# A two-layer graph network on one core: where VectorE doubles the low part, and the order of a step around it

## The chip, the core and the metric

The kernel runs on one core of a Trainium2 chip. The time is the device time of one execution in microseconds, from the kernel's median of several runs; the trace comes from one profiled execution, whose clock starts with its first instruction. TensorE does the matrix products, VectorE, ScalarE and GpSimd the element-wise work, SyncE issues the loads and stores. Each engine runs its own list of instructions in order, and semaphores tie the lists together.

## What is computed

128 graphs of 64 nodes with 512 features in fp32, and one adjacency matrix of 64 x 64:

```python
x = layernorm(x + einsum('bnf,nm->bmf', x, adj * adj) + bias)
z_l, z_g, v = x @ W_lang.T, x @ W_grav.T, x @ W_V.T
A_l = max(cosine(z_l, z_l), 0) * not_eye
A_g = exp(-dist2(z_g, z_g) / (2 sigma**2)) * not_eye
K = w_l * rownorm(A_l * adj) + (1 - w_l) * rownorm(A_g * adj)
x = layernorm(x + (K @ v) @ W_O.T)
```

## The kernel before

The 128 graphs go through in 16 groups of 8 (512 rows, as four tiles of 128 x 512), one group g a step. A step is a software pipeline: while it computes the projections, the Gram matrices and K of group g, it also brings group g+1 through the first layer and its transposes, and closes group g-1 (K·u, the sum with the residual, the second layer norm, the store). The order on each engine is written out by hand in a function `step(g)` for each engine, with a prologue before step 0 and a last step written out separately. Nothing plans it: an instruction that waits holds everything behind it on its engine.

Products are made in three terms from a high and a low part of each operand (hi·hi, hi·lo, lo·hi). So each transposed tile of the normalised y is kept three times: `hT` (the full value, copied by ScalarE, `copy_hT`), `hT_hi` (rounded, by ScalarE, `hi_hT`) and `hT_lo` (their difference, by VectorE, `lo_hT`, L780). The buffers alternate between two groups.

TensorE's step: the products 0 to 3 of the projections (L388), the two halves of layer 0 of group g+1 (`layer0`, L348) alternating with the two halves of K·u of group g-1 (`apply_k`, L439), products 4 to 8, the transposes of tiles 0 and 1 of group g+1 (`transpose_h`, L361), the Gram products (`gram`, L407), then products 9, 10, 11 with the transposes of tiles 2 and 3 between, and two small transposes of the inverse norms (`rows`, L419). Products 8 to 11 are u, the product with the folded W_V and W_O. Three PSUM banks form a ring for the products; ScalarE empties them (`evict`). The last tile of layer 0 sits in a ring bank too, and product 6 is the next to take that bank, once VectorE has added the bias (`add_y`, L764). The second half of K·u writes the banks that the first two of these additions read.

`gram(g)` multiplies `hT` with the projections. For its first chunk it needs hT + hT_lo in place of hT, which VectorE makes in place (`double_lo`, L786) and counts in `hT_doubled`; gram waits for it at L395. In the kernel before VectorE does it for group g+1 at the end of step g, behind `turn_k(g)` (L880, K's transposition) and in front of `add_y(g + 2, 0)`.

VectorE's step begins with the additions of y and z (`add_y`, `add_z` L886) and their statistics (`count_y`, `count_z` L891, `gather_z` L900). Then it waits for ScalarE's copy of P, gram's result (`copy_p`), and goes down a long chain: `diagonals` (L791), `lo_hT` of tiles 0 and 1, `shift`, `turn_p` (L815), `lo_hT` of tiles 2 and 3, `add_p` (L822), `weigh` (L831, needs TensorE's `rows`), `coefficients`, `combine`, `turn_k`. GpSimd makes the scale and offset of the layer norms from the statistics (`scale_y`, `scale_z`, with L1079 to L1084) and the inverse norms (`columns`); ScalarE applies them (`normalise_h`, `normalise_out`).

Of the kernel before, what the change touches and what calls it, by code (L numbers as in the profile page):

```python
# [5 lines left out]
def bass_two_layer_graph_resnorm(  # L6
# [64 lines left out]
    with ctx:  # L71
# [243 lines left out]
        def _(pe):  # L315
# [127 lines left out]
            def step(g, tail=True):  # L443
                project(g, 0)
                project(g, 1)
                project(g, 2)
                project(g, 3)
                layer0(g + 1, 0)
                if tail:
                    apply_k(g - 1, 0)  # L450
                layer0(g + 1, 1)
                if tail:
                    apply_k(g - 1, 1)
                project(g, 4)
                project(g, 5)
                project(g, 6)
                project(g, 7)
                project(g, 8)
                transpose_h(g + 1, 0)
                transpose_h(g + 1, 1)  # L460
                gram(g)
                project(g, 9)
                transpose_h(g + 1, 2)
                project(g, 10)
                transpose_h(g + 1, 3)
                project(g, 11)
                rows(g)
# [85 lines left out]
            g = NG - 1  # L553
# [20 lines left out]
        def _(act):  # L574
# [8 lines left out]
            def normalise_h(g, p):  # L583
                act.wait_ge(y_scale, 2 * g + p // 2 + 1)
                act.activation(h_sb[g % 3][:, p, :], h_sb[g % 3][:, p, :], ACT.Identity, scale=y_rs[:, p:p + 1],  # L585
                               bias=y_nb[:, p:p + 1]).then_inc(h_ready, 1)
# [33 lines left out]
            def step(g, tail=True):  # L620
                evict(g, 0)
                evict(g, 1)
                evict(g, 2)
                evict(g, 3)
                evict(g, 4)
                evict(g, 5)
                normalise_h(g + 1, 0)
                normalise_h(g + 1, 1)
                evict(g, 6)
                evict(g, 7)  # L630
                normalise_h(g + 1, 2)
                evict(g, 8)
                if tail:
                    normalise_out(g - 1, 0)
                hi_hT(g + 1, 0)
                copy_hT(g + 1, 0)
                copy_p(g)
                hi_hT(g + 1, 1)
                normalise_h(g + 1, 3)
                copy_hT(g + 1, 1)  # L640
                evict(g, 9)
                copy_hT(g + 1, 2)
                evict(g, 10)
                hi_hT(g + 1, 2)
                hi_hT(g + 1, 3)
                copy_hT(g + 1, 3)
                if tail:
                    normalise_out(g - 1, 1)
                exp_g(g)
                if tail:  # L650
                    normalise_out(g - 1, 2)
                    normalise_out(g - 1, 3)
                evict(g, 11)
# [73 lines left out]
            g = NG - 1  # L727
# [23 lines left out]
        def _(dve):  # L751
# [151 lines left out]
            def step(g, tail=True):  # L903
                add_y(g + 1, 0)
                add_y(g + 1, 1)
                if tail:
                    add_z(g - 1, 0)
                    count_z(g - 1, 0)
                add_y(g + 1, 2)
                if tail:  # L910
                    add_z(g - 1, 1)
                    count_z(g - 1, 1)
                add_y(g + 1, 3)
                if tail:
                    gather_z(g - 1, 0)
                    add_z(g - 1, 2)
                count_y(g + 1, 0)
                count_y(g + 1, 1)
                if tail:
                    add_z(g - 1, 3)  # L920
                    count_z(g - 1, 2)
                    count_z(g - 1, 3)
                diagonals(g)
                lo_hT(g + 1, 0)
                lo_hT(g + 1, 1)
                shift(g)
                turn_p(g)
                if tail:
                    gather_z(g - 1, 1)
                lo_hT(g + 1, 2)  # L930
                lo_hT(g + 1, 3)
                add_p(g)
                weigh(g)
                coefficients(g)
                combine(g)
                turn_k(g)
                double_lo(g + 1)

            def blocks_of_ident():
                dve.wait_ge(ident_ready, 2)  # L940
# [85 lines left out]
            lo_hT(0, 2)  # L1026
            lo_setup(13)
            lo_hT(0, 3)
            double_lo(0)
            lo_setup(14)  # L1030
            lo_setup(15)

# [1 line left out]
            for g in range(1, NG - 1):  # L1034
                step(g)
            g = NG - 1
            add_z(g - 1, 0)
            count_z(g - 1, 0)
            add_z(g - 1, 1)
# [5 lines left out]
            add_p(g)  # L1045
            weigh(g)
            coefficients(g)
            add_z(g - 1, 3)
            combine(g)
            gather_z(g - 1, 0)  # L1050
            turn_k(g)
            count_z(g - 1, 2)
            count_z(g - 1, 3)
            gather_z(g - 1, 1)
            add_z(g, 0)
            add_z(g, 1)
            count_z(g, 0)
            count_z(g, 1)
            add_z(g, 2)
            gather_z(g, 0)  # L1060
# [11 lines left out]
        @block.gpsimd  # L1072
        def _(pool):
            def scale_of(stats, ve_done, rs_done, scale, mv, ve, nm, rs, nb, d, h):

                pq = slice(2 * h, 2 * h + 2)
                pool.wait_ge(stats, d + 1)
                settle(pool)
                pool.tensor_scalar(ve[:, pq], mv[:, pq, 1], LN_EPS, None, ALU.add).then_inc(ve_done, 1)  # L1079
                pool.wait_ge(ve_done, d + 1)  # L1080
                pool.tensor_tensor(rs[:, pq], ve[:, pq], pow_neg_half[:, 0:2], ALU.pow).then_inc(rs_done, 1)
                pool.tensor_scalar(nm[:, pq], mv[:, pq, 0], -1.0, None, ALU.mult).then_inc(rs_done, 1)
                pool.wait_ge(rs_done, 2 * d + 2)
                pool.tensor_tensor(nb[:, pq], nm[:, pq], rs[:, pq], ALU.mult).then_inc(scale, 1)  # L1084

            def scale_y(g, h):
                scale_of(y_stats, y_ve_done, y_rs_done, y_scale, y_mv, y_ve, y_nm, y_rs, y_nb, 2 * g + h, h)

            def scale_z(g, h):
                if g > 0:  # L1090
                    pool.wait_ge(o_ready, NP * g - NP + 2 * h + 2)
                scale_of(z_stats, z_ve_done, z_rs_done, z_scale, z_mv, z_ve, z_nm, z_rs, z_nb, 2 * g + h, h)

            def columns(g):
                pool.wait_ge(sq_done, g + 1)
                settle(pool)

                pool.tensor_scalar(sq_floor[:, :].rearrange("r (h a) -> r h a", a=2), sq[:, :, L, :], EPS * EPS, None,
                                   ALU.max).then_inc(floor_done, 1)
                pool.wait_ge(floor_done, g + 1)  # L1100
                pool.tensor_tensor(inv_norm[:, :], sq_floor[:, :], pow_neg_half[:, :], ALU.pow).then_inc(inv_done, 1)
                pool.tensor_scalar(sq_eps[:, :], sq_floor[:, :], 2 * EPS, None, ALU.mult).then_inc(sq_eps_done, 1)
                pool.wait_ge(inv_done, g + 1)
                pool.tensor_copy(inv_rep[:, :, :], inv_norm[:, :].unsqueeze(2).broadcast_to([R, NP, N])).then_inc(
                    inv_ready, 1)
                pool.wait_ge(sq_eps_done, g + 1)
                pool.tensor_tensor(floors[:, L, :], sq_eps[:, :], inv_norm[:, :], ALU.mult).then_inc(floors_ready, 1)

            def step(g, tail=True):
                scale_y(g + 1, 0)  # L1110
                scale_y(g + 1, 1)
                if tail:
                    scale_z(g - 1, 0)
                columns(g)
                if tail:
                    scale_z(g - 1, 1)

            pool.memset(ident[:, :], 0.0).then_inc(ident_ready, 1)
            pool.wait_ge(ident_ready, 1)
            pool.affine_select(out=ident[:, :], in_=ident[:, :], compare_op=ALU.not_equal, fill=1.0, base=0,  # L1120
                               pattern=[[-1, R]], channel_multiplier=1).then_inc(ident_ready, 1)
            pool.memset(pow_neg_half[:, :], -0.5)
            pool.memset(floors[:, G, :], EPS).then_inc(pow_ready, 1)
            pool.wait_ge(pow_ready, 1)
            for h in range(2):
                scale_y(0, h)
            step(0, tail=False)
            for g in range(1, NG - 1):
                step(g)
            g = NG - 1  # L1130
            columns(g)
            scale_z(g - 1, 0)
            scale_z(g - 1, 1)
            scale_z(g, 0)
            scale_z(g, 1)
# [27 lines left out]
```

## Time and profile before

| | before |
|---|---|
| median of 3 runs | 600.31 us (599.86 to 600.78) |
| the profiled execution | 600.05 us, span 598.2 us |
| TensorE busy | 578.7 us (97%), clock 0.995 of full |
| VectorE busy | 439.0 us (73%) |
| ScalarE busy | 292.1 us (49%) |
| GpSimd busy | 141.2 us (24%) |
| one step | about 34.3 us |

"Busy" adds up the times in which an engine has an instruction under way. The ends of matrix products are modelled and overlap with the next one's start, so distances between starts say more about TensorE than durations do. PEld is TensorE's weight load.

### The profile page before, as it was taken

How to read it: one execution, taken by the hardware profiler on the slowest of the kernel's cores; microseconds unless marked ns; L12 is line 12 of the kernel's file. 1: busy time of each engine (PE TensorE's matmuls, PEld its weight loads, DVE VectorE, ACT ScalarE, POOL GpSimd, SP SyncE). 2: the span in 40 equal slices, each digit the busy share in tenths (PEclk: the TensorE clock that was granted, in tenths of full speed). 3: DMA queues.
4: the chain of work that ended last, by engine and by line, in shares of the span. 5: the costliest groups of instructions: out<-in, count | busy, mean ns of one | idle time of the engine just before them, and what ended most of it. 6: DMA issues, size and time to landing. Idle time of an engine off the chain costs nothing.

```text
span 598.2 us, 10012 instructions
## 1 busy us (share of the span) xinstructions
PE 578.7 (97%) x3681; PEld 443.2 (74%) x3681; DVE 439.0 (73%) x1022; ACT 292.1 (49%) x516; POOL 141.2 (24%) x344
## 2 busy tenths in 40 slices
PE   7999999999999999999999999999999999999991
PEld 5887868686886868688686868778686868868770
DVE  4843795959689595959769595967959595886586
ACT  4644426365463635456362645546263644636413
POOL 0201113032232304123230313223130412323013
PEclk9999999999999999999999999999999999999997
DMA  8713030411313040131304022131303110100003
GB/s 297 196 21 70 1 71 19 96 46 54 89 53 71 26 116 20 54 87 55 71 37 105 19 85 58 54 85 58 71 19 108 35 54 19 53 1 37 36 0 140
DMA packets 20783, 38.67 MB, mean 65 GB/s; under 512 B 2176, under 2 KB 2176, under 8 KB 20736
## 3 DMA queue, kind: packets, MB, share of 16 engines
q1 hardware_dynamic: 20736, 38.05, 22.4%
q8 instruction: 29, 0.48, 0.3%
q14 instruction: 18, 0.15, 0.1%
HBM read 21.27 MB, written 16.78 MB: 64 GB/s over the span
## 4 chain that ended last, share of the span: by engine, by line
PE 61%; DVE 27%; ACT 5%; issue 4%; DMA 1%; SPq 0%; DVEq 0%; POOL 0%; POOLq 0%
PE ring L388 42%; PE bank_s L407 10%; DVE KT L880 5%; DVE h_sb L764 3%; DVE X L831 3%; PE bank_y L439 3%; ACT hT_hi L576 2%; PE bank_y L361 2%; DVE XW L860 2%; DVE sums L845 2%; DVE hT_lo L780 2%; DVE S L822 2%; PE ring L513 1%; ACT u_sb L576 1%; PE bank_z L361 1%
## 5 line engine op out<-in xcount | busy, mean ns | idle before, releaser
L576 ACT ACTIVATE yT<-ring 128x512 f32<-128x512 f32 x128 | 71.0, 592 | 141.5 <-PE ring L388 141.4
L388 PE MATMUL ring<-hT_hi,T_hi 128*128 128x512 f32 x320 | 127.7, 399 | 0.0
L388 PE MATMUL ring<-hT_hi,T_lo 128*128 128x512 f32 x320 | 124.8, 390 | 0.0
L388 PE MATMUL ring<-hT_lo,T_hi 128*128 128x512 f32 x288 | 112.3, 390 | 0.0
L388 PE MATMUL ring<-M_hi,hT_hi 128*128 128x512 f32 x256 | 104.5, 408 | 0.0
L388 PE MATMUL ring<-M_hi,hT_lo 128*128 128x512 f32 x256 | 100.4, 392 | 0.0
L388 PE MATMUL ring<-M_lo,hT_hi 128*128 128x512 f32 x256 | 99.8, 390 | 0.0
L791 DVE TENSOR_TENSOR diag_scr<-P_sb,ident_c 128x512 f32<-128x512 f32 x16 | 11.1, 692 | 103.4 <-ACT P_sb L576 103.4
L388 PEld LDWEIGHTS ring<-hT_hi,T_hi 128*128 128x128 f32 x320 | 60.0, 188 | 23.8 <-issue 12.2
L1079 POOL TENSOR_SCALAR y_ve<-y_mv 128x2 f32<-128x2 f32 x32 | 7.7, 239 | 266.2 <-DVE y_mv L774 265.0
L585 ACT ACTIVATE h_sb<-h_sb,y_nb,y_rs 128x512 f32<-128x512 f32 x64 | 50.4, 810 | 39.6 <-POOL y_nb L1084 39.6
L388 PEld LDWEIGHTS ring<-hT_hi,T_lo 128*128 128x128 f32 x320 | 60.1, 188 | 12.8
L388 PEld LDWEIGHTS ring<-hT_lo,T_hi 128*128 128x128 f32 x288 | 54.2, 188 | 10.4
L576 ACT ACTIVATE u_sb<-ring 128x512 f32<-128x512 f32 x64 | 37.7, 590 | 44.6 <-PE ring L388 44.6
L407 PE MATMUL bank_s<-yT,hT 128*64 128x128 f32 x1024 | 59.4, 274 | 0.0
L407 PEld LDWEIGHTS bank_s<-yT,hT 128*64 128x64 f32 x1024 | 55.6, 137 | 3.3 <-issue 1.8
L815 DVE STREAM_TRANSPOSE P_turned<-P_sb 32x256 f32<-32x256 f32 x128 | 55.8, 436 | 2.0
L388 PEld LDWEIGHTS ring<-M_hi,hT_hi 128*128 128x128 f32 x256 | 48.1, 188 | 11.8 <-issue 3.4
L388 PEld LDWEIGHTS ring<-M_hi,hT_lo 128*128 128x128 f32 x256 | 48.0, 188 | 10.7
L388 PEld LDWEIGHTS ring<-M_lo,hT_hi 128*128 128x128 f32 x256 | 48.2, 188 | 8.7
L617 ACT ACTIVATE h_sb<-h_sb,z_nb,z_rs 128x512 f32<-128x512 f32 x63 | 49.6, 811 | 8.0 <-POOL z_nb L1084 7.9
L780 DVE TENSOR_TENSOR hT_lo<-hT,hT_hi 128x512 fp32r<-128x512 f32 x64 | 42.3, 680 | 4.5 <-ACT hT L576 4.2
(135 smaller groups left out, 849.0 us busy)
## 6 DMA issues: line engine op xcount, KB each, us to landing
x_sb<-in_x_dram SPq DMA_DIRECT2D x32, 512.0 KB, 6.4
out_dram<-h_sb SPq DMA_DIRECT2D x60, 256.0 KB, 2.0
yT<-in_L_gnn_W_lang_dram SPq DMA_DIRECT2D x4, 256.0 KB, 3.1
yT<-in_L_gnn_W_grav_dram SPq DMA_DIRECT2D x1, 1024.0 KB, 7.4
h_sb<-in_L_gnn_W_V_dram SPq DMA_DIRECT2D x1, 1024.0 KB, 11.0
h_sb<-in_L_gnn_W_O_dram SPq DMA_DIRECT2D x1, 1024.0 KB, 12.4
out_dram<-h_sb SPq DMA_DIRECT2D x8, 128.0 KB, 2.4
bias_bc<-in_L_gnn_bias_dram SPq DMA_DIRECT2D x1, 256.0 KB, 8.2
```

The lines of the kernel that those rows point to most:

```text
L361: last = pe.transpose(hT_bank[p][:, s], h_sb[g % 3][:, p, s], ident[:, :])
L388: last = pe.matmul(ring[ring_of(g, k)][:, :], a, b, start=n == 0, stop=n == len(terms) - 1)
L407: last = pe.matmul(p_ps[half(a), h, :, c, :], hT[g % 2][:, i, t], yT[:, i, :, t], start=i == 0, stop=i == DC - 1, tile_position=(0, a * N))
L439: last = pe.matmul(z_bank(2 * h + a)[half(c), :], KT[half(a), h, half(c)], u_sb[half(a), 2 * h + c, :], start=True, stop=True, tile_positi ...
L576: return act.activation(dst, src, ACT.Copy, scale=scale)
L585: act.activation(h_sb[g % 3][:, p, :], h_sb[g % 3][:, p, :], ACT.Identity, scale=y_rs[:, p:p + 1], bias=y_nb[:, p:p + 1]).then_inc(h_ready, 1)
L617: act.activation(h_sb[g % 3][:, p, :], h_sb[g % 3][:, p, :], ACT.Identity, scale=z_rs[:, p:p + 1], bias=z_nb[:, p:p + 1]).then_inc(o_ready, 1)
L764: dve.tensor_tensor(h_sb[g % 3][:, p, :], y_bank(g, p)[:, :], bias_bc[:, :], ALU.add).then_inc(y_added, 1)
L780: dve.tensor_tensor(hT_view(hT_lo[g % 2], p), hT_view(hT[g % 2], p), hT_view(hT_hi[g % 2], p), ALU.subtract).then_inc(hT_split, 1)
L815: last = dve.transpose(P_turned[col:col + B, :, i * B:(i + 1) * B], P_sb[row:row + B, :, :, :, j * B:(j + 1) * B].rearrange("r h s a j -> ...
L831: last = dve.scalar_tensor_tensor(X0[half(a), :, c, :], S2[half(a), :, L, c, :], 0.0, row_ps[half(c), :, half(a)], ALU.max, ALU.mult)
L880: last = dve.transpose(K_t[col:col + B, :, i * B:(i + 1) * B], K_sb[row:row + B, :, j * B:(j + 1) * B])
```

## The change

VectorE's `double_lo` leaves the end of the step (and the prologue) and stands in the step of the same group, behind `count_y(g + 1, 1)`. In the same edit other orders of the step are changed: on TensorE transposition 2 comes directly behind gram; on ScalarE evictions 6 and 8 come ahead of the normalisations of y beside them, and copy and conversion of the transposed tiles 1 and 2 are reordered; on VectorE `gather_z(g - 1, 0)` goes ahead of the last `add_y`, the last `add_z` between the two counts of y, `lo_hT(g + 1, 0)` ahead of `diagonals`, `count_z(g - 1, 3)` behind `shift`; on GpSimd z's first scale between y's two. The last step gets small moves of the gatherings and counts of z. No operation is added or taken away.

```diff
--- before.py
+++ after.py
@@ -459,8 +459,8 @@
                 transpose_h(g + 1, 0)
                 transpose_h(g + 1, 1)
                 gram(g)
+                transpose_h(g + 1, 2)
                 project(g, 9)
-                transpose_h(g + 1, 2)
                 project(g, 10)
                 transpose_h(g + 1, 3)
                 project(g, 11)
@@ -625,23 +625,23 @@
                 evict(g, 4)
                 evict(g, 5)
                 normalise_h(g + 1, 0)
+                evict(g, 6)
                 normalise_h(g + 1, 1)
-                evict(g, 6)
                 evict(g, 7)
+                evict(g, 8)
                 normalise_h(g + 1, 2)
-                evict(g, 8)
                 if tail:
                     normalise_out(g - 1, 0)
                 hi_hT(g + 1, 0)
                 copy_hT(g + 1, 0)
                 copy_p(g)
+                copy_hT(g + 1, 1)
                 hi_hT(g + 1, 1)
                 normalise_h(g + 1, 3)
-                copy_hT(g + 1, 1)
                 evict(g, 9)
                 copy_hT(g + 1, 2)
+                hi_hT(g + 1, 2)
                 evict(g, 10)
-                hi_hT(g + 1, 2)
                 hi_hT(g + 1, 3)
                 copy_hT(g + 1, 3)
                 if tail:
@@ -910,20 +910,23 @@
                 if tail:
                     add_z(g - 1, 1)
                     count_z(g - 1, 1)
+                    gather_z(g - 1, 0)
                 add_y(g + 1, 3)
                 if tail:
-                    gather_z(g - 1, 0)
                     add_z(g - 1, 2)
                 count_y(g + 1, 0)
+                if tail:
+                    add_z(g - 1, 3)
                 count_y(g + 1, 1)
-                if tail:
-                    add_z(g - 1, 3)
+                double_lo(g)
+                if tail:
                     count_z(g - 1, 2)
-                    count_z(g - 1, 3)
+                lo_hT(g + 1, 0)
                 diagonals(g)
-                lo_hT(g + 1, 0)
                 lo_hT(g + 1, 1)
                 shift(g)
+                if tail:
+                    count_z(g - 1, 3)
                 turn_p(g)
                 if tail:
                     gather_z(g - 1, 1)
@@ -934,7 +937,6 @@
                 coefficients(g)
                 combine(g)
                 turn_k(g)
-                double_lo(g + 1)
 
             def blocks_of_ident():
                 dve.wait_ge(ident_ready, 2)
@@ -1026,7 +1028,6 @@
             lo_hT(0, 2)
             lo_setup(13)
             lo_hT(0, 3)
-            double_lo(0)
             lo_setup(14)
             lo_setup(15)
 
@@ -1034,6 +1035,7 @@
             for g in range(1, NG - 1):
                 step(g)
             g = NG - 1
+            double_lo(g)
             add_z(g - 1, 0)
             count_z(g - 1, 0)
             add_z(g - 1, 1)
@@ -1045,16 +1047,16 @@
             add_p(g)
             weigh(g)
             coefficients(g)
+            gather_z(g - 1, 0)
             add_z(g - 1, 3)
             combine(g)
-            gather_z(g - 1, 0)
             turn_k(g)
             count_z(g - 1, 2)
             count_z(g - 1, 3)
+            add_z(g, 0)
             gather_z(g - 1, 1)
-            add_z(g, 0)
+            count_z(g, 0)
             add_z(g, 1)
-            count_z(g, 0)
             count_z(g, 1)
             add_z(g, 2)
             gather_z(g, 0)
@@ -1108,9 +1110,9 @@
 
             def step(g, tail=True):
                 scale_y(g + 1, 0)
+                if tail:
+                    scale_z(g - 1, 0)
                 scale_y(g + 1, 1)
-                if tail:
-                    scale_z(g - 1, 0)
                 columns(g)
                 if tail:
                     scale_z(g - 1, 1)
```

## Rows read from the trace of the kernel before

**Rows 1.** one whole step by engine (stretch, us, busy and instructions, PEclk, DMA, GB/s)
```profile
252.83:287.14 34.31, 34.13 (x220) 26.06 (x221) 26.29 (x62) 17.25 (x30) 8.79 (x21) 1.00 0.23 63
```

**Rows 2.** list of waits (who <- whom: us in total, times, longest)
```profile
PE bank_y L439 <- DVE h_sb L764: 2.6, 14, 0.2
DVE diag_scr L791 <- ACT P_sb L576: 103.4, 16, 10.0
```

**Rows 3.** timeline of TensorE, turn of a step (start us, us, engine, what, count)
```profile
249.73 1.09 PE L348 MATMUL bank_y<-x_sb,mix 64*64 64x512 f32 x8
...
250.69 1.09 PE L439 MATMUL bank_z<-u_sb,KT 64*64 64x512 f32 x8
...
251.60 0.59 PE L348 MATMUL bank_s<-x_sb,mix 64*64 64x512 f32 x1
...
252.83 1.09 PE L439 MATMUL bank_y<-u_sb,KT 64*64 64x512 f32 x8 [0.19 <-DVE h_sb L764]
...
253.85 0.50 PE L388 MATMUL ring<-hT_hi,T_hi 128*128 128x512 f32 x1
```

**Rows 4.** timeline of TensorE, the same place in step 0, without K·u
```profile
45.65 1.09 PE L348 MATMUL bank_y<-x_sb,mix 64*64 64x512 f32 x8
...
46.56 0.59 PE L348 MATMUL bank_s<-x_sb,mix 64*64 64x512 f32 x1
...
47.53 0.50 PE L388 MATMUL ring<-hT_hi,T_hi 128*128 128x512 f32 x1
```

**Rows 5.** timeline of VectorE, from K's turning to z's counts
```profile
248.12 2.52 DVE L880 STREAM_TRANSPOSE KT<-K_sb 32x128 f32<-32x128 f32 x8
...
250.67 0.69 DVE L786 TENSOR_TENSOR hT<-hT,hT_lo 128x512 f32<-128x512 f32 x1
...
251.39 1.29 DVE L764 TENSOR_TENSOR h_sb<-bank_y,bias_bc 128x512 f32<-128x512 f32 x2
...
255.84 0.67 DVE L764 TENSOR_TENSOR h_sb<-ring,bias_bc 128x512 f32<-128x512 f32 x1
...
260.80 1.28 DVE L891 BATCH_NORM_STATS2 z_bn<-h_sb 128x6 f32<-128x512 f32 x2
```

**Rows 6.** timeline of TensorE, product 6, gram, transposition 2, product 10, norms' transposes
```profile
257.15 0.39 PE L388 MATMUL ring<-hT_hi,T_hi 128*128 128x512 f32 x1
...
264.24 3.71 PE L407 MATMUL bank_s<-yT,hT 128*64 128x128 f32 x64
...
270.75 0.60 PE L361 MATMUL bank_z<-ident,h_sb 128*128 128x128 f32 x4
...
271.42 0.39 PE L388 MATMUL ring<-M_lo,hT_hi 128*128 128x512 f32 x1
...
277.14 0.38 PE L419 MATMUL bank_y<-ident,inv_rep 128*128 128x128 f32 x2
```

**Rows 7.** timeline of VectorE behind gram: diagonals, lo(0) and lo(1), lo(3), weighing
```profile
268.63 0.69 DVE L791 TENSOR_TENSOR diag_scr<-P_sb,ident_c 128x512 f32<-128x512 f32 x1 [6.55 <-ACT P_sb L576]
...
269.96 1.28 DVE L780 TENSOR_TENSOR hT_lo<-hT,hT_hi 128x512 fp32r<-128x512 f32 x2
...
276.31 0.69 DVE L780 TENSOR_TENSOR hT_lo<-hT,hT_hi 128x512 fp32r<-128x512 f32 x1 [0.25 <-ACT hT L576]
...
277.71 1.18 DVE L831 SCALAR_TENSOR_TENSOR X<-S,bank_y 64x128 f32<-64x128 f32 x4
```

**Rows 8.** timeline of ScalarE: copy of transposition 0, copy of P
```profile
265.35 0.60 ACT L576 ACTIVATE hT<-bank_y 128x512 f32<-128x512 f32 x1
...
268.00 0.60 ACT L576 ACTIVATE P_sb<-bank_s 128x512 f32<-128x512 f32 x1 [2.05 <-PE bank_s L407]
```

**Rows 9.** timeline of GpSimd: scale of z's first half, first operation of the second
```profile
262.35 0.22 POOL L1079 TENSOR_SCALAR z_ve<-z_mv 128x2 f32<-128x2 f32 x1
...
263.76 0.20 POOL L1084 TENSOR_TENSOR z_nb<-z_nm,z_rs 128x2 f32<-128x2 f32 x1
...
275.63 0.51 POOL L1079 TENSOR_SCALAR z_ve<-z_mv 128x2 f32<-128x2 f32 x1 [2.65 <-issue]
```

More of the change, by code:

```diff
@@ L912, in step @@
                     count_z(g - 1, 1)
+                    gather_z(g - 1, 0)
                 add_y(g + 1, 3)
                 if tail:
-                    gather_z(g - 1, 0)
                     add_z(g - 1, 2)
                 count_y(g + 1, 0)
-                count_y(g + 1, 1)
                 if tail:
                     add_z(g - 1, 3)
+                count_y(g + 1, 1)
+                double_lo(g)
+                if tail:
                     count_z(g - 1, 2)
-                    count_z(g - 1, 3)
+                lo_hT(g + 1, 0)
                 diagonals(g)
-                lo_hT(g + 1, 0)
                 lo_hT(g + 1, 1)
                 shift(g)
+                if tail:
+                    count_z(g - 1, 3)
                 turn_p(g)
@@ L1110, in step @@
                 scale_y(g + 1, 0)
-                scale_y(g + 1, 1)
                 if tail:
                     scale_z(g - 1, 0)
+                scale_y(g + 1, 1)
                 columns(g)
```

## The prediction

> **What bounds the kernel now.** I read the stages first: in the stretch of one whole step TensorE is busy for 34.13 of 34.31 us at full granted clock, VectorE for 26.29, ScalarE for 17.25, GpSimd for 8.79 [rows 1]. So the steady state belongs to TensorE, and another engine can cost time only where TensorE waits for it. The list of waits shows where: fourteen times the second half of K·u (L439 into bank_y) waits for the sums of y (L764) [rows 2]. VectorE itself has 103.4 us of idle time, nearly all before the diagonals, where it waits for ScalarE's copy of P [rows 2].
>
> The listed 2.6 us (0.19 each) understates that wait, because modelled ends overlap; starts are better. In a steady step layer0's first half starts at 249.73, K·u's first half at 250.69, layer0's second at 251.60, K·u's second at 252.83, the next product at 253.85 [rows 3]. The spacings are 0.96, 0.91, 1.23, 1.02. All three first ones have the same four tiled matrix products ahead. Step 0 has layer0's two halves without K·u: 0.91 apart, and 0.97 to the next product [rows 4]. So 0.91 is the unhindered spacing: **the second K·u loses 1.23 - 0.91 = 0.32 us, the first 0.96 - 0.91 = 0.05 us**, in 14 steps.
>
> Who is late? VectorE turns K from 248.12 to 250.64, just ahead of the first K·u's 250.69, doubles the low part from 250.67, adds y from 251.39 (two additions, 1.29, ending 252.68); K·u starts at 252.83 [rows 5]. The doubling stands squarely in that chain, and layer0's result has been there since 249.73 + 1.09 = 250.82.
>
> **The change, part by part.** *The doubling taken out behind K's turning.* One operation, from 250.67 to 251.39 start to start: 0.72 us per step [rows 5]. Not all of it comes back: the additions of y must now wait for layer0's end at 250.82, and would start at about 250.88 instead of 251.39, 0.51 earlier. They would end at 252.17, and K·u, with the same 0.15 between, could start at 252.32. TensorE itself is ready at 251.60 + 0.91 = 252.51. So the wait goes altogether, with 0.19 to spare: 14 x 0.32 = 4.5 us.
>
> *The doubling put behind the sums of y and z.* The sums end when the last counts of z do, at 260.80 + 1.28, and then VectorE is idle to 268.63 [rows 5, 7]. The doubling's reader is gram, at 264.24 [rows 6]. In the new order it comes at about 260.4 (260.80 before, less 0.51 for the earlier start, 0.1 for a gap ahead of the gathering) and ends at 261.1. Gram then comes 0.37 earlier, at 263.9. Cover of 2.8 us: cost nothing. If that cover were gone, gram would wait for every microsecond.
>
> *Lo of transposition 0 ahead of the diagonals, the last count of z behind the shift.* These swap two pieces between the idle stretch and the chain behind gram. Lo(0) needs ScalarE's copy, which ends at 265.35 + 0.60 = 265.95; P's copy is at 268.00 after 2.05 of idleness [rows 8]. It fits before the diagonals. What it gives up in the chain (half of 1.28 [rows 7]) the count of z takes (half of 1.28 [rows 5]). The count also fills the gap between the shift and the turning of P, some 0.1. Net 0 to -0.1.
>
> *ScalarE's order and transposition 2 directly behind gram.* Lo(3) waited 0.25 for ScalarE's copy [rows 7]; with the conversion of transposition 2 done before, ScalarE reaches transposition 3 one operation (about 0.5 us) earlier, and this wait should go. The chain is then stopped elsewhere: the weighing (277.71) needs the two transposes of the norms that TensorE starts at 277.14 and ends at 277.52 [rows 6, 7]. Allowing 0.07, it can start at 277.59, only 0.12 earlier. K is then turned at 250.64 - 0.12 = 250.52 in the other step's clock, and the first K·u can start at its unhindered 250.64: 0.05 x 14 = 0.7 us. This term is thin: its bounds are 0 and 0.7 us, and I take the upper, because the releasing transposes have the same place before K·u on TensorE as before.
>
> For TensorE the move of transposition 2 is the same work in another place. Its turn from the products of step 9 into it and back disappears, one from gram into it is new, which no row shows. Four transposes start at 270.75 and the second matrix product behind them at 271.42 [rows 6]; less the 0.23 that one takes (14 of them from 253.85 to 257.15 [rows 3, 6]) that is 0.44, or 0.11 a transpose, with no fee of the turn visible. I take 0; bounds -0.1 to +0.1 in 15 steps: -1.5 to +1.5 us. The evictions and normalisations of y swap among themselves; ScalarE has 2.05 us of idleness ahead of P's copy [rows 8], which covers them. The conversions and the store queue behind them move by less than 1 us; the stores have no reader.
>
> *The gathering of z ahead of the last addition of y.* That addition empties the ring bank which product 6 takes, at 257.15 [rows 6]. It ends at 255.84 + 0.67 = 256.51 [rows 5]. The gathering costs 0.16 and a gap of 0.1, the earlier start gives 0.51: 256.26. Product 6 comes at 257.15 - 0.37 = 256.78. Margin 0.5: nothing.
>
> *GpSimd: z's scale between y's two.* Z's scale takes from 262.35 to 263.96 [rows 9] right behind y's second; with the two exchanged and the earlier start, y's second is ready at about 263.6. ScalarE now wants it behind product 8's eviction, an estimate of also 263.6 (product 8 ends ahead of gram's transposes), and transposition 2 wants the result only behind gram. Behind it ScalarE has four pieces up to the copy for lo(0), which then ends at about 266.4; lo(0) has to start by 268.63 - 0.37 - 0.6 = 267.7. Nothing, up to 1.3 us of delay. Here a row bears on the doubling's new place: a 128x2 operation of GpSimd takes 0.22 us at 262.35 and 0.51 at 275.63, when VectorE is in a subtraction of two SBUF tensors [rows 9]. The doubling is such an operation too, and is moved beside GpSimd's scales, which were alone before. It may hold them by 0.3 us, or up to its own 0.7, within the 1.3. The Trainium skill (SBUF — State Buffer, Who interferes with whom) states that a VectorE instruction with two SBUF inputs and a GpSimd instruction that reads SBUF exclude each other for a whole instruction, whichever comes first. The two rows agree; by the rule the sum stays, and the slower rival below gets a part of its chance.
>
> *Prologue and last step.* The doubling before the last two splits of the setup goes; TensorE was not waiting there (the list names no such wait for VectorE's L974), so 0. In the last step the doubling stays where it was. There a gathering moves from behind K's sum, where it partly fills a gap between two dependent operations, to ahead of an addition that fills one already: +0.1 us on the last chain, bounds 0 and the 0.25 of a gathering.
>
> **Sum.** Against the profiled execution, 600.05 us (span 598.2 and 1.85 around it): 600.05 - 4.5 - 0.7 + 0.1 = 594.95. The median of the three runs, 600.31, is 0.26 above the profiled one: **595.2 us**.
>
> **Rivals.**
> *The margin is used up at product 6 or at the transposes.* If the gathering holds the last addition of y for 0.7 us instead of 0.26 (or y's scales come late), TensorE waits 0.2 more in 14 steps, +2.8: 598.0. Against it: 0.5 us margin, and the sum above needs only half of it.
> *The change does not do what it says:* the 1.23 is a property of the switch from layer0's second half (two banks) to K·u. Then only the 0.05 comes back: 599.6. Against it: layer0's second half is followed after 0.97 in step 0 [rows 4], and the list names L764 as the releaser. For it: K·u never follows layer0's second half unhindered in this trace.
> *Slower:* lo(0), now ahead of the diagonals, isn't done when P is copied, because ScalarE (held by GpSimd's later second scale) has not copied transposition 0. Then both lo(0) and the count of z lie in the chain behind gram, 0.6 longer: K turned at 251.12, first K·u at 251.17, 0.53 late instead of 0.37 for both halves together. That is +0.16 x 14 = 2.2, with the tail 602.6. It decides from a ScalarE about 1.3 us late (first delay) and is complete at 1.9. For it: diagonals queue behind lo(0) with no way round. Against it: the idleness of 2.05 us.
>
> **How the numbers follow.** Forecast 0.72, margin used up 0.13, no effect 0.09, slower 0.06. A measurement of this kernel can tell about 0.2% (1.2 us) from no change; so faster 0.85, same 0.09, slower 0.06. The forecast's own bounds: 595.2 - 1.5 = 593.7, and 595.2 + 1.5 + 0.7 = 597.4. For 8 in 10 I reach a little into the rival at 598.0: 593.5 to 598.0.
>
> **What would show it.** Right: the wait of L439 for L764 is gone; starts inside the block of layer0 and K·u are 0.91 apart, the block from 249.73 to 253.85 (4.12) takes about 3.75; a steady step is 33.9 to 34.0 instead of 34.3; the doubling runs at about 9 us into the step with gram not waiting; diagonals still wait for P's copy. Wrong: a spacing above 1.1 before the second K·u (no effect), a wait of product 6 for L764 (margin), a wait of K·u for L880 of over 0.2 or diagonals behind lo(0) (slower), a step shorter or longer by 0.1 in the stretch from gram to product 10 (the transposes' turn).

## The result and the profile after

The changed kernel takes 591.95 us (median of four runs, 591.32 to 593.11), the kernel before in the same comparison 600.09 us. The ratio is 0.9866 with a 95% interval of 0.9847 to 0.9884: faster by 8.1 us, where 5.1 were forecast, and below the stated range of 593.5 to 598.0. The sign and the mechanism were right, the size was not.

The profiled execution took 591.92 us, its span is 590.1. One whole step of it by engine, with the columns of [rows 1]:

```profile
249.50:283.25 33.75, 33.75 (x224) 26.11 (x224) 26.22 (x62) 17.58 (x30) 8.76 (x21) 1.00 0.23 64
```

A steady step has gone from 34.3 to 33.75 us, and TensorE now shows no idle time in it at all; its granted clock is 1.00 as before. From the second K·u of step 1 to that of step 14 the trace takes 439.03 us (80.47 to 519.50), where before it took 446.78 (80.83 to 527.61): 7.75 of the 8.1 us lie there, 0.60 a step. Up to the first one it is 0.36 less. From that last K·u to the end it is 70.60 against 70.59. That stretch holds two things: up to the norms' transposes of step 14 it is 0.10 shorter (24.21 against 24.31), and from there to the end about 0.1 longer (46.39 against 46.28; the spans are given to 0.1).

The list of waits, to be read against [rows 2] (who <- whom: us in total, times, longest):

```profile
DVE hT_lo L780 <- ACT hT L576: 76.1, 17, 6.6
DVE diag_scr L791 <- ACT P_sb L576: 14.2, 16, 2.1
...
DVE h_sb L764 <- PE bank_y L348: 11.6, 14, 6.3
...
PEld bank_z L439 <- DVE KT L880: 11.5, 15, 2.8
...
DVE X L831 <- PE bank_y L419: 5.3, 15, 0.4
```

K·u's wait for y's sums, fourteen times before, is gone. In its place y's sums wait for TensorE (L764 for L348), and so does the weighing (L831 for L419). Most of VectorE's idle time before the diagonals is now in front of lo(0), the making of the low part of tile 0: 76.1 us at L780 and 14.2 still at the diagonals.

The block of layer 0 and K·u on TensorE, to be read against [rows 3] (timeline, start us, us, what):

```profile
246.87 1.09 PE L348 MATMUL bank_y<-x_sb,mix 64*64 64x512 f32 x8
247.78 1.04 PE L439 MATMUL bank_z<-u_sb,KT 64*64 64x512 f32 x8
248.64 0.59 PE L348 MATMUL bank_s<-x_sb,mix 64*64 64x512 f32 x1
...
249.50 1.06 PE L439 MATMUL bank_y<-u_sb,KT 64*64 64x512 f32 x8
250.48 0.50 PE L388 MATMUL ring<-hT_hi,T_hi 128*128 128x512 f32 x1
```

The four spacings (each from one start to the next) are 0.91, 0.86, 0.86, 0.98 against 0.96, 0.91, 1.23, 1.02: the block takes 3.61 us instead of 4.12, 0.51 less. The fourth, from the second K·u to the product behind it, is called the exit below. I had forecast 0.37, with three of the spacings at 0.91.

TensorE from gram on, against [rows 6]:

```profile
260.90 3.71 PE L407 MATMUL bank_s<-yT,hT 128*64 128x128 f32 x64
264.55 0.66 PE L361 MATMUL bank_z<-ident,h_sb 128*128 128x128 f32 x4
264.96 0.47 PE L388 MATMUL ring<-M_hi,hT_hi 128*128 128x512 f32 x1
...
270.51 0.60 PE L361 MATMUL bank_z<-ident,h_sb 128*128 128x128 f32 x4
...
273.71 0.38 PE L419 MATMUL bank_y<-ident,inv_rep 128*128 128x128 f32 x2
```

Gram takes 3.65 in both. From its end to the norms' transposes it is 9.16 us (264.55 to 273.71), where before it was 277.14 - (264.24 + 3.65) = 9.25: another 0.09 a step. Together 0.60, the whole gain of a step; the 41 products between the two places take between 10.39 and 10.44 us in either trace.

VectorE's part of the same step, against [rows 5, 7]:

```profile
245.10 2.52 DVE L880 STREAM_TRANSPOSE KT<-K_sb 32x128 f32<-32x128 f32 x8
248.03 1.29 DVE L764 TENSOR_TENSOR h_sb<-bank_y,bias_bc 128x512 f32<-128x512 f32 x2 [0.41 <-PE bank_y L348]
...
257.70 0.66 DVE L786 TENSOR_TENSOR hT<-hT,hT_lo 128x512 f32<-128x512 f32 x1
258.27 0.69 DVE L891 BATCH_NORM_STATS2 z_bn<-h_sb 128x6 f32<-128x512 f32 x1
263.83 0.69 DVE L780 TENSOR_TENSOR hT_lo<-hT,hT_hi 128x512 fp32r<-128x512 f32 x1 [4.87 <-ACT hT L576]
265.29 0.69 DVE L791 TENSOR_TENSOR diag_scr<-P_sb,ident_c 128x512 f32<-128x512 f32 x1 [0.77 <-ACT P_sb L576]
...
271.93 1.26 DVE L780 TENSOR_TENSOR hT_lo<-hT,hT_hi 128x512 fp32r<-128x512 f32 x2
...
274.13 1.19 DVE L831 SCALAR_TENSOR_TENSOR X<-S,bank_y 64x128 f32<-64x128 f32 x4 [0.34 <-PE bank_y L419]
```

K is turned at 247.62, 0.16 before the first K·u at 247.78; before, K·u started 0.05 or 0.06 behind K's turning in all 14 steps. The doubling ends at 258.36, 2.5 us ahead of gram's 260.90. Lo(2) and lo(3) run without a gap, and the weighing waits 0.34 for TensorE.

### The profile page after: what moved, and what is told of

Its sections match the earlier page's. It is cut to its first block, busy times and chain, and to the rows that moved or that the text cites. A ratio compares the mean times of both kernels' runs of the same rounds, so it can differ in the third digit from the quotient of the medians.

```text
span 590.1 us, 10012 instructions
## 1 busy us (share of the span) xinstructions
PE 574.5 (97%) x3681; PEld 445.5 (75%) x3681; DVE 437.9 (74%) x1022; ACT 296.8 (50%) x516; POOL 140.5 (24%) x344
## 4 chain that ended last, share of the span: by engine, by line
PE 93%; DVE 4%; issue 1%; DMA 1%; ACT 0%; POOL 0%; SPq 0%; POOLq 0%; DVEq 0%
PE ring L388 63%; PE bank_s L407 10%; PE bank_z L361 3%; PE bank_y L348 3%; PE bank_y L361 2%; PE bank_z L439 2%; PE bank_s L348 2%; PE bank_y L439 2%; PE ring L490 2%; PE ring L513 1%; DVE KT L880 1%; DVE z_bn L891 1%; DMA yT<-in_L_gnn_W_lang_dram 1%; DVE P_turned L815 1%; PE bank_y L419 1%
## 5 line engine op out<-in xcount | busy, mean ns | idle before, releaser
L576 ACT ACTIVATE yT<-ring 128x512 f32<-128x512 f32 x128 | 72.6, 593 | 138.0 <-PE ring L388 138.0
L388 PE MATMUL ring<-M_hi,hT_hi 128*128 128x512 f32 x256 | 102.7, 401 | 0.0
L780 DVE TENSOR_TENSOR hT_lo<-hT,hT_hi 128x512 fp32r<-128x512 f32 x64 | 42.3, 681 | 76.2 <-ACT hT L576 76.1
L585 ACT ACTIVATE h_sb<-h_sb,y_nb,y_rs 128x512 f32<-128x512 f32 x64 | 52.1, 815 | 50.1 <-POOL y_nb L1086 50.1
L1081 POOL TENSOR_SCALAR y_ve<-y_mv 128x2 f32<-128x2 f32 x32 | 7.6, 237 | 264.9 <-DVE y_mv L774 263.6
L891 DVE BATCH_NORM_STATS2 z_bn<-h_sb 128x6 f32<-128x512 f32 x64 | 44.0, 690 | 1.1
```

Source lines behind the costliest of these rows:

```text
L388: last = pe.matmul(ring[ring_of(g, k)][:, :], a, b, start=n == 0, stop=n == len(terms) - 1)
L576: return act.activation(dst, src, ACT.Copy, scale=scale)
L780: dve.tensor_tensor(hT_view(hT_lo[g % 2], p), hT_view(hT[g % 2], p), hT_view(hT_hi[g % 2], p), ALU.subtract).then_inc(hT_split, 1)
L891: dve.bn_stats(z_bn[:, p, :], h_sb[g % 3][:, p, :]).then_inc(z_counted, 1)
```

## The experiments

The theory after seeing the two traces had three parts. (1) The doubling's old place gave the second K·u's wait. (2) K is turned a little earlier, by one of the other exchanges, and this gives the 0.05 of the first K·u and another 0.05 behind it, since a group that started behind a wait makes the next start 0.05 later. (3) The place of transposition 2 gives 0.09. The rival is that the gain hangs on the new order as a whole. Times are medians, the ratios are against the kernel before; "block" means the four spacings above. The edits are shown in part.

### only_doubling: the doubling alone, in the kernel before

```diff
                     count_z(g - 1, 3)
+                double_lo(g)
                 diagonals(g)
...
                 turn_k(g)
-                double_lo(g + 1)
```

> The kernel before with one edit: the doubling stands behind the counts of z (and at the head of the last step), all other orders as before. Theory 1 (the doubling sat in the chain K turned, y added, second K·u): the second K·u's spacing falls from 1.22 to 0.86 and its exit from 1.02 to 0.98, while the first K·u stays at 0.96 and the half behind it at 0.91, since K is turned no earlier: 0.40 x 14 = 5.6 us, about 594.5 us. Rival (the gain comes from the other orders, and the doubling's place alone only shifts the wait to K's turning): under 1.5 us, 598.6 us or more, with the first K·u now at 1.1 or above.

595.04 us (594.85 to 595.78), ratio 0.9914 (0.9901 to 0.9928). The block of a steady step:

```profile
248.97 1.09 PE L439 MATMUL bank_z<-u_sb,KT 64*64 64x512 f32 x8
249.88 0.59 PE L348 MATMUL bank_s<-x_sb,mix 64*64 64x512 f32 x1
...
250.74 1.04 PE L439 MATMUL bank_y<-u_sb,KT 64*64 64x512 f32 x8
```

The block has about 0.95, 0.91, 0.86, 0.97 in most steps, a steady step is 33.95. So the doubling's place alone brings 5.4 us, two thirds of the gain, and it leaves the first K·u where it was. The second K·u's wait was 0.37, not 0.32. Here the doubling stands behind the last counts of z, a little later than in the change.

### doubling_back: the whole change without the doubling's move

```diff
                 turn_k(g)
+                double_lo(g + 1)
...
                 count_y(g + 1, 1)
-                double_lo(g)
```

> The changed kernel with the doubling again behind K's turning (and in the prologue), all other orders as changed. Theory 1: y's additions start 0.36 later (K turned at 247.62 plus 0.72, against 248.03 now), the second K·u 0.33 later, and a group behind a wait costs 0.05 more: +0.38 x 14 = +5.3 us, about 597.3 us, with the first K·u still at 0.91. Rival (the other orders have made enough room that the doubling is hidden behind layer0 anyway): 592 to 593 us.

597.24 us (596.59 to 597.77), ratio 0.9948 (0.9935 to 0.9960). The block:

```profile
248.97 1.09 PE L348 MATMUL bank_y<-x_sb,mix 64*64 64x512 f32 x8
249.88 1.04 PE L439 MATMUL bank_z<-u_sb,KT 64*64 64x512 f32 x8
250.74 0.59 PE L348 MATMUL bank_s<-x_sb,mix 64*64 64x512 f32 x1
...
251.91 1.09 PE L439 MATMUL bank_y<-u_sb,KT 64*64 64x512 f32 x8
```

The first K·u stays unhindered, the second is 1.17 behind layer 0's second half instead of 0.86, and the product behind it 1.02 instead of 0.98. A steady step is 34.11. With all the other exchanges in place the doubling still costs 5.3 us in its old place, about what it costs alone. The rival, a gain that hangs on the new order as a whole, has fallen.

### t2_back: the whole change with transposition 2 behind product 9

```diff
-                transpose_h(g + 1, 2)
                 project(g, 9)
+                transpose_h(g + 1, 2)
```

> The changed kernel with transposition 2 again behind product 9 on TensorE, everything else as changed. Theory (a turn from transposes back into full products costs about 0.1 us, and the change saved one of them a step): gram's end to the norms' transposes goes from 9.16 to 9.25 us, +0.09 x 15 = +1.3 us, 593.3 us. Rival (the turn is free, as the prediction took it, and the missing gain lies in the layer0 and K·u block): 592.0 us, same as the changed kernel, with 9.16 in that stretch.

594.04 us (593.10 to 594.45), ratio 0.9894 (0.9878 to 0.9909). The block is as in the changed kernel. A steady step is 33.86 against 33.75: 0.11. The first product of step 0 starts at 39.55 in this trace and at 39.14 in that of the changed kernel, so about 0.4 of the 2.1 us between the medians is the start, before any line that differs.

### doubling_t2 and doubling_t2_hi2: building the change up from the kernel before

```diff
                 gram(g)
+                transpose_h(g + 1, 2)
                 project(g, 9)
-                transpose_h(g + 1, 2)
```

on top of only_doubling makes doubling_t2. On top of that, doubling_t2_hi2 has on ScalarE

```diff
                 copy_hT(g + 1, 2)
+                hi_hT(g + 1, 2)
                 evict(g, 10)
-                hi_hT(g + 1, 2)
                 hi_hT(g + 1, 3)
```

> The kernel before with two parts of the change: the doubling behind the counts of z, and transposition 2 directly behind gram on TensorE. ScalarE, GpSimd and the rest of VectorE keep the order of before. Theory (the two act apart; K is still turned as late as before, so the first K·u stays at 0.95 and the half behind it at 0.91): 595.0 of the doubling alone less 0.09 x 15 = 593.7 us. Rival (transposition 2 earlier also brings K earlier, since ScalarE has its tile sooner): 592.0 us, with the first K·u at 0.91 and the next at 0.86.

> As doubling_t2, with one more part of the change: ScalarE makes the rounded copy of transposition 2 ahead of evicting product 10 instead of behind it. Theory (this single exchange removes the 0.25 us that lo(3) waited, the weighing is then held by TensorE's transposes of the norms alone, K is turned 0.15 earlier, and the first K·u and the half behind it give 0.05 each): 0.10 x 14 = 1.4 less than doubling_t2, 592.2 us, the time of the whole change; the remaining edits are worth nothing. Rival (VectorE's and GpSimd's exchanges are needed as well): 593.7 us.

doubling_t2 took 592.84 us (592.00 to 593.60), doubling_t2_hi2 591.65 us (590.75 to 592.60). The first product of step 0 starts at different times in these traces (39.13 with the doubling alone, 38.79, 39.14), so the steady steps are the better measure: 33.95 with the doubling alone, 33.83 with transposition 2 as well, 33.73 with ScalarE's exchange as well, and 33.75 in the whole change. With transposition 2 alone the first K·u and the half behind it stay at 0.96 and 0.91; with ScalarE's exchange they become 0.91 and 0.86. On VectorE, lo(3) in doubling_t2, and then lo(2) with lo(3) and the weighing in doubling_t2_hi2:

```profile
273.09 0.69 DVE L780 TENSOR_TENSOR hT_lo<-hT,hT_hi 128x512 fp32r<-128x512 f32 x1 [0.17 <-ACT hT L576]
```

```profile
272.01 1.26 DVE L780 TENSOR_TENSOR hT_lo<-hT,hT_hi 128x512 fp32r<-128x512 f32 x2
...
274.08 1.19 DVE L831 SCALAR_TENSOR_TENSOR X<-S,bank_y 64x128 f32<-64x128 f32 x4 [0.21 <-PE bank_y L419]
```

Lo(3)'s wait for ScalarE goes, and the weighing waits for TensorE in its place. Three edits make the whole steady gain; the other exchanges on VectorE, ScalarE and GpSimd are worth nothing that these runs can show. Nor does the first K·u need transposition 2's new place: in t2_back, which has the other exchanges without it, the block is that of the changed kernel.

### kt_late: K turned later by a known amount, in the changed kernel

```diff
                 dve.wait_ge(xw_done, g + 1)
+                dve.tensor_tensor(diag_scr[:, 0:NP, :], XW[:, L, :, :], XW[:, G, :, :], ALU.add)
```

> The changed kernel with one needless addition of 128x256 into a scratch tile ahead of K's sum, in every step: K is turned 0.34 later, at 247.96 in the step where it was 247.62, and the first K·u can start at 248.01 instead of 247.78, 0.23 late. Theory (a group that starts behind a wait costs the group behind it 0.05 on top, 0.91 instead of 0.86): 0.28 x 14 = 3.9, plus 0.34 in the last step, 596.2 us. Rival (a wait costs its own length and no more): 0.23 x 14 + 0.34 = 3.6, 595.5 us, with the half behind the first K·u at 0.86.

596.32 us (595.79 to 597.37), ratio 0.9942 (0.9929 to 0.9955). The block of a steady step:

```profile
247.94 1.09 PE L348 MATMUL bank_y<-x_sb,mix 64*64 64x512 f32 x8
249.08 1.09 PE L439 MATMUL bank_z<-u_sb,KT 64*64 64x512 f32 x8
249.99 0.59 PE L348 MATMUL bank_s<-x_sb,mix 64*64 64x512 f32 x1
...
250.85 1.04 PE L439 MATMUL bank_y<-u_sb,KT 64*64 64x512 f32 x8
```

The first K·u is 1.14 behind, 0.23 late as forecast; the half behind it takes 0.91 instead of 0.86 in all 14 steps, the second K·u 0.86. So a wait costs its length and 0.05 more. At the exit 0.01 or 0.02 comes back, and the step is 34.00, 0.25 longer rather than 0.28. Two steps were longer still by 0.12 and 0.35, where VectorE itself came late; so it is partly luck that the total met the forecast of 596.2 so closely. The 0.91 in all 14 steps decides against the rival, the total alone does not.

### rows_early: the norms' transposes behind transposition 3

```diff
                 transpose_h(g + 1, 3)
+                rows(g)
                 project(g, 11)
-                rows(g)
```

> The changed kernel with the two transposes of the norms directly behind transposition 3 instead of behind product 11. Theory (a turn from transposes into full products costs about 0.09 us, and this removes another one in 15 steps): -1.3 us, 590.6 us; the weighing's wait of 0.34 for TensorE goes, K is turned about 0.3 earlier, which buys nothing more except in step 2, whose first K·u was 0.25 late. Rival (turns are free): 591.7 us. Second rival (the inverse norms come too late from GpSimd, and TensorE waits at their transposes): slower than 592 us.

591.33 us (591.24 to 591.47), ratio 0.9850 (0.9837 to 0.9864). A steady step is 33.70, 0.05 less than in the changed kernel, not 0.09. Against the kernel before it is faster; against the changed kernel (591.95) the 0.6 us lies within what the runs can tell. The four transposes now take 0.44 instead of 0.36 when others follow (270.51 to 270.95), so 0.08 of the 0.13 that the joined products save is given back there. Step 2, whose first K·u came 1.16 behind in the changed kernel, has it at 0.97: the weighing no longer waits for TensorE, and the earlier K buys something only there. What is late in step 2 is one small operation of VectorE in K's chain (L851, behind the reduction L845): it starts about 0.5 us late with no other engine named as the reason, in step 2 of every kernel here but kt_late. Its cause stays open.

### rows_tail: the last step reordered, on top of rows_early

```diff
             project(g, 4)
+            apply_k(g - 1, 0)
+            apply_k(g - 1, 1)
...
             project(g, 7)
-            apply_k(g - 1, 0)
             gram(g)
-            apply_k(g - 1, 1)
```

with all sums and counts of z of group 14 ahead of the diagonals on VectorE, and GpSimd's scales of that group ahead of the inverse norms.

> The kernel of rows_early with the last step reordered: both halves of K·u of group 14 behind product 4 instead of around gram, so that VectorE does all sums and counts of z of group 14 while it would wait for P, and none of them in the chain behind gram. Theory: two additions (0.6 each), two gatherings (0.3 together) leave that chain, and the second K·u ahead of gram costs 0.9: -0.6 to -0.8 us, about 590.6 us. Rival (ScalarE or GpSimd ends later, or the two K·u before gram cost more than they give): 591.3 us or more.

591.55 us (591.07 to 592.28): by the medians the same as rows_early, and not the 590.6 of the theory. VectorE's chain from the diagonals to K turned did get shorter, from 14.82 us (562.18 to 577.00) to 13.64 (563.80 to 577.44), but gram started later (559.41 against 557.78):

```profile
559.41 3.71 PE L407 MATMUL bank_s<-yT,hT 128*64 128x128 f32 x64 [0.69 <-ACT yT L576]
```

Counted from the norms' transposes of step 14 (540.34 here, 540.55 there), gram starts 19.07 instead of 17.23 us behind, 1.84 later. One K·u more ahead of it is 0.9, and 0.69 is the wait for the eviction of product 7, which K·u had hidden in its old place; the rest was not traced. From those transposes to the end it is 49.8 us against 49.2, so this last step is slower by 0.6; that the medians agree doesn't show it.

## Why the prediction was right in kind and wrong in size

**What bounds the kernel, and where it waits.** Right. The doubling stood in the chain from K turned through y's sums to the second K·u; the wait went, as the list of waits and only_doubling show.

**The new place of the doubling.** Right: nothing waits for it. It was to end at 261.1 against a gram at 263.9; it ends 2.5 us ahead of gram. Lo(0) fits before the diagonals with 0.77 to spare, so the slower rival did not occur, though 1.3 had been forecast. Product 6 shows no wait either, so the margin was not used up; but its addition ends at 253.52 (252.86 + 0.66) and product 6 starts at 253.80, a margin of 0.28 instead of 0.5. The rival "the change does not do what it says" fell with the spacing of 0.86.

**The unhindered spacing, first mis-sized term.** The step that failed is "So 0.91 is the unhindered spacing". I took 0.91 from layer 0's two halves in step 0 and from the group behind the first K·u. Both were poor yardsticks: the first group comes directly behind full-size products, and the other starts behind a wait. A tiled group behind one that has neither cause comes after 0.86. The term 1.23 - 0.91 = 0.32 should have been 0.37, the 0.05 behind the first K·u was missing altogether, and the exit, which the forecast left at 1.02, gives 0.04: the block gains 0.51 a step, not 0.37. Over 14 steps that is 0.14 x 14 = 2.0 of the missing 3.0 us. kt_late shows the extra 0.05 behind a wait that was made on purpose; why TensorE takes it was not tried.

**The first K·u's 0.05.** Right in kind, and the chain was followed rightly: lo(3)'s wait goes, and the weighing is then held by the norms' transposes. What I called thin (0.12 earlier) held in every step but step 2. That it hangs on ScalarE's exchange is shown by doubling_t2_hi2 against doubling_t2.

**Transposition 2, second mis-sized term.** Taken at 0, bounds -1.5 to +1.5 us; measured 0.09 to 0.12 a step in three pairs of kernels, 1.4 to 1.8 us of gain over 15 steps. The step that failed was "no fee of the turn visible": I spread the 0.44 over four transposes and concluded that the turn was free. One more reading of the trace before could have told otherwise:

```profile
267.89 0.50 PE L388 MATMUL ring<-M_hi,hT_hi 128*128 128x512 f32 x1
...
271.10 0.47 PE L388 MATMUL ring<-M_hi,hT_hi 128*128 128x512 f32 x1
...
273.94 0.60 PE L361 MATMUL bank_z<-ident,h_sb 128*128 128x128 f32 x4
```

The transposes take 0.35 (270.75 to 271.10), and the first product behind them 0.32 (to 271.42) where the later ones take 0.23: the 0.44 held a fee of 0.09. Products 9 and 10 with the transposition between them took 2.86 and 2.84; joined they take 5.55 in the changed kernel, 0.15 less, of which the transposition behind gram takes back 0.06 (0.41 instead of 0.35). rows_early shows that the same joining elsewhere saves only 0.05 net. So it is no fixed price, and my second theory of 0.09 for every turn fell too. With the block's 2.0 the two terms give 3.4 us where 3.0 were missing; the later start of step 0 (39.14 against 38.96) takes back 0.2, and the rest is within the spread of the runs.

**The range.** I gave transposition 2 bounds on both sides, and the block none below its forecast. That made the range too high. The trace before had a shorter spacing inside one half of layer 0, whose second round starts 0.43 behind the first at 251.60:

```profile
252.03 0.59 PE L348 MATMUL bank_s<-x_sb,mix 64*64 64x512 f32 x1
```

Two rounds of 0.43 are 0.86. As a bound for the second K·u and for the half behind the first it would have given 0.10 more a step, and the 0.97 that [rows 4] show behind layer 0, as a bound for the exit, another 0.05: 14 x 0.15 = 2.1 us off the lower end, and the median would have lain inside.

**GpSimd beside the doubling.** As the rows had suggested, GpSimd's power beside it took longer, 1.10 us where it takes 0.72 in the same step a scale earlier:

```profile
256.12 0.72 POOL L1083 TENSOR_TENSOR y_rs<-y_ve,pow_neg_half 128x2 f32<-128x2 f32 x1
...
257.82 1.10 POOL L1083 TENSOR_TENSOR z_rs<-z_ve,pow_neg_half 128x2 f32<-128x2 f32 x1
```

It is 1.10 or 1.11 in 13 of the 14 steps; in step 2, where the two are shifted against each other, the operation ahead of it has the excess instead (L1081, 0.56 for 0.22). By the Trainium skill (SBUF — State Buffer, Who interferes with whom) a VectorE instruction with two SBUF inputs, as the doubling is, contends with a GpSimd instruction that reads SBUF; the trace agrees, with 0.38 us. ScalarE then waits 0.51 for y's second scale, all within its slack, as forecast: no effect on the time.

**The last step.** Forecast +0.1, measured about +0.1 from the norms' transposes of step 14 to the end (46.39 against 46.28). The last first K·u comes 0.19 later behind its products (10.81 us instead of 10.62, 566.68 to 577.49); in doubling_t2_hi2, whose last step keeps the order of before, it is 10.62.

## What to carry to other kernels

When the bounding engine waits in short spots, look in the chain that releases it for an operation whose result isn't wanted there, and move it to where its engine idles; the gain is the wait, not the operation's length (0.72 moved, 0.4 gained). Take the unhindered spacing of a group from a place where neither it nor the group before it has waited and both are of the same kind, or from its own rounds, and add what the group behind a wait loses. A group of small products between full-size ones has a price at its borders that depends on both neighbours: measure it by the length of the whole stretch, joined and apart.

## What the runs showed of the hardware that I had not expected

A group of four tiled products (64x64 tiles, 512 columns, in eight records) that starts behind a wait makes the next one start after 0.91 us; behind an unhindered one that itself follows such a group, the next starts after 0.86. Layer 0's first half, which comes behind full-size products, is followed after 0.91 though nothing waits. The difference of 0.05 was there in 14 of 14 steps of kt_late and of the kernel before, and in step 2 of the changed kernel, the only one of its 14 in which the first K·u was late. Behind a second K·u that had waited, the next product starts after 1.02 instead of 0.98. Four transposes between full-size products take 0.35 or 0.36 us to the next start, directly behind gram 0.41, and 0.44 when other transposes follow.
